# Last feed-forward stage: token scale moved into TensorE's turning, rounding constant taken off on ScalarE, normalisation on GpSimd

## The chip, the cores and the metric

One core of one Trainium2 chip. The metric is device time in microseconds of one execution of the whole program.

## The reference, cut to what matters

Eight layers (four attentions, four feed-forwards) work on `x` of 8 batches of 256 tokens of 256 values. The change is in the last layer, a feed-forward with quantised tokens, quantised weights and a depthwise convolution along the tokens:

```python
def act_quant(x):
    scale = 127.0 / jnp.clip(jnp.max(jnp.abs(x), axis=-1, keepdims=True), 1e-05)
    return jnp.clip(jnp.round(x * scale), -128, 127) / scale
...
h = bit_linear(x, w1)                                   # act_quant(x) @ weight_quant(w1).T
h = depthwise_conv1d(h.transpose(0, 2, 1), conv_w, conv_b)   # three taps along the tokens
h = h.transpose(0, 2, 1)
h = jax.nn.silu(h)
return bit_linear(h, w2)
...
x = x + _L3_ffn_ref(_layernorm(x, axis=-1), ...)
```

## The kernel before, in words

`build` runs the layers one after the other as stages; the last is `bit_ffn` (from line 2511). It works on one batch (256 tokens, two tiles of 128) at a time, in a pipeline of 12 steps. In step n, five batches are in work at once, each at another part of the layer:

- **batch n (new)**: VectorE normalises the two tiles (`norm`, line 2606, tile `xn`), takes the largest absolute value of each token (`token_scale`, line 2613, `amax`), makes of it the unit `qr` (line 2617) and its inverse `qs` (2619). ScalarE multiplies by `qs` and adds MAGIC = 1.5 x 2^23, which rounds to a whole number (`rounded`, 2714, `q1`).
- **batch n-1 (turn)**: VectorE takes MAGIC off and multiplies by `qr` (`unrounded`, 2627, `q2`, two instructions). TensorE turns the tokens (`turn_tokens`, 2808, `px`), ScalarE writes the high part (`high_part`, 2721, `xh`), VectorE the rest (`low_part`, 2632, `xl`).
- **batch n-2 (hid)**: for each of 8 groups f of 128 hidden channels TensorE multiplies (`hidden`, 2820, into one of three banks of `ph`), ScalarE applies the middle tap of the convolution (`middle_tap`, 2728), VectorE the first and the last (`first_tap` 2637, `last_tap` 2642, `y`). A bank is free again after its last tap. After f = 3 and f = 7 ScalarE applies the silu to half of the channels (`silu`, 2736, `sT`).
- **batch n-3 (end)**: for each of its two tiles TensorE turns the result (`turn_silu`, 2831, into the one buffer `pn`), VectorE finds the scale (`tile_scale`: 2651 `sax`, 2658 `sunit`, 2662 `sqs`), then `pn` is scaled and rounded to `s1`: tile 0 by ScalarE (`scaled`, 2743), tile 1 by VectorE (`scaled_late`, 2669, last in its step). GpSimd takes MAGIC off (`whole`, 2786 and 2790, `sq`). TensorE turns it back (`turn_back`, 2840, `pb`).
- **batch n-4 (last)**: ScalarE copies `pb` to `sqT` (`turned_back`, 2751), TensorE multiplies with the second weight (`product`, 2849, `po`), VectorE scales and adds it to `x` (`residual`, 2675). SyncE stores it.

Each engine runs its own list of a step in the order written out in its `step` function; nothing else orders the work, and every engine waits in order on semaphores. VectorE's list has 17 places: place 2f is the first tap of f, place 2f+1 its last tap, and the other operations are put at places:

```python
if turn and place < TB: unrounded(...)        # in front of the taps 0 and 1
if end and 3 <= place < 6: tile_scale(0)      # in front of the tap
if last and place in (6, 10): residual(...)
if new and place in (5, 6): norm(...)
if turn and place == 7: low_part(...)
if new and place in (9, 10, 12): token_scale(...)
```

ScalarE's and TensorE's lists go by f. TensorE, in front of `hidden(f)`: f = 2 `turn_silu` of tile 0; f = 3 `turn_tokens`, then `turn_back` of tile 1; f = 4 `product` of tile 0; f = 5 `product` of tile 1; f = 6 `turn_silu` of tile 1; `turn_back` of tile 0 at the end. ScalarE: f = 0 middle tap, `turned_back` of tile 0; f = 3 middle tap, `turned_back` of tile 1, `high_part`; f = 4 middle tap, `scaled`, `silu` of the first half; f = 7 middle tap, `rounded`, `silu` of the second half. Steps 0 to 3 and 8 to 11 are written out, 4 to 7 are a loop of two passes. Step 8 has no new batch, step 9 nothing to turn either, step 10 no hidden part, step 11 only the last part.

## Time and profile before

| | us |
|---|---|
| median of 3 runs | 1684.4 (1680.64 to 1686.13) |
| the profiled execution | 1677.31 |
| its span | 1675.4 |
| last feed-forward stage within the span | from 1529.7 to the end |
| VectorE busy in the span | 960.2 (57%) |
| TensorE, ScalarE, GpSimd busy | 1453.5, 648.3, 424.8 |
| granted TensorE clock, mean | 0.945 |

The span is the time from the first to the last instruction of the profiled execution. All times of the rows below are counted from its start. A timeline gives start, duration, engine, source line and tiles of each piece; a square bracket holds the idle time of the engine before it, and what ended it. The ends of matmuls are modelled, and a following matmul may start before them. VectorE's and ScalarE's instructions overlap by about 0.1 us too, so the distance of two starts is what one costs its engine.

### The profile page before, as it was taken

The page shows a single profiled execution, that of the slowest core. Times are in us where ns is not written, and L with a number is a line of the kernel's source. Part 1 is how long each engine was busy: PE and PEld are TensorE (multiplying, and loading weights), DVE is VectorE, ACT ScalarE, POOL GpSimd, SP SyncE. Part 2 cuts the span into 40 slices and gives each one's busy share as a digit, 9 for nine tenths or more (in the row PEclk, how much of TensorE's full clock was granted, in tenths as well). Part 3 has the DMA queues.
Part 4 walks back from the last instruction along what each step waited for, and adds up shares of the span by engine and source line. Part 5 has one row for each costly group of instructions (what it writes and reads, how often), then busy time and mean ns, then how long its engine had stood idle before and what let it go on. Part 6 is the DMA issues. An engine that isn't in the chain of part 4 may idle for free. (4 is left out here: it accounts for less than half of the span.)

```text
span 1675.4 us, 32751 instructions
## 1 busy us (share of the span) xinstructions
PE 1453.5 (87%) x11594; PEld 1275.4 (76%) x11594; DVE 960.2 (57%) x2376; ACT 648.3 (39%) x1422; POOL 424.8 (25%) x671
## 2 busy tenths in 40 slices
PE   4789998399986999999998789999999988885775
PEld 3456665389985788888887689999999986664664
DVE  4666763312213676666666565555555546776995
ACT  1233333022213444554544144444444422234773
POOL 2011101134304344344333011100000016650222
PEclk8899999599997999999999899999999999998897
...
DMA packets 97293, 139.82 MB, mean 83 GB/s; under 512 B 10080, under 2 KB 81248, under 8 KB 97056
## 3 DMA queue, kind: packets, MB, share of 16 engines
...
## 5 line engine op out<-in xcount | busy, mean ns | idle before, releaser
L1872 PE MATMUL f_ph<-f_xgT,f_w 128*128 128x128 f32 x2496 | 287.0, 276 | 2.8 <-ACT f_xgT L1906 2.3
L1872 PEld LDWEIGHTS f_ph<-f_xgT,f_w 128*128 128x128 f32 x2496 | 283.8, 193 | 3.4 <-issue 1.8
L1031 ACT ACTIVATE a_work<-a_ps,a_bias 128x128 f32<-128x128 f32 (+1 forms) x256 | 104.3, 420 | 172.2 <-issue 90.6
L1953 DVE TENSOR_TENSOR f_w_low<-f_w,f_w_high 128x2048 fp32r<-128x2048 f32 x39 | 89.4, 2293 | 99.8 <-ACT f_w_high L1912 99.8
L1231 POOL TENSOR_TENSOR a_work<-a_work,a_recip 128x256 f32<-128x256 f32 (+1 forms) x128 | 103.3, 829 | 146.9 <-DVE a_recip L1150 145.8
...
L574 DVE CUSTOM_DVE_ANT_0 a_shut_s<-a_ps,a_neg 128x256 f32<-128x256 f32 x256 | 93.1, 420 | 39.9 <-PE a_ps L253 39.3
L486 ACT ACTIVATE a_pT<-a_ps 128x1024 f32<-128x1024 f32 x64 | 65.6, 1025 | 119.4 <-PE a_ps L253 119.4
L1912 ACT ACTIVATE f_w_high<-f_w 128x2048 fp32r<-128x2048 f32 x39 | 74.5, 1910 | 85.4 <-DVE f_yg L1965 85.4
L1155 DVE TENSOR_TENSOR a_qk<-a_ps,a_qk 128x512 fp32r<-128x512 f32 x64 | 44.3, 692 | 96.8 <-ACT a_qk L1048 96.8
L1674 PEld LDWEIGHTS f_ph<-f_xgT,f_w 128*128 128x128 f32 x736 | 87.3, 195 | 6.5 <-DMA f_w<-in_f_w 4.0
L1674 PE MATMUL f_ph<-f_xgT,f_w 128*128 128x128 f32 x736 | 88.3, 279 | 3.6 <-DMA f_w<-in_f_w 2.7
L1883 PE MATMUL f_py<-f_w_high,f_h_high 128*128 128x256 f32 x312 | 91.4, 293 | 0.0
L1883 PE MATMUL f_py<-f_w_high,f_h_low 128*128 128x256 f32 x312 | 88.1, 282 | 0.0
L1958 DVE TENSOR_TENSOR f_h_low<-f_raw,f_h_high 128x512 fp32r<-128x512 f32 x78 | 56.9, 729 | 54.4 <-ACT f_h_high L1916 54.4
L1883 PE MATMUL f_py<-f_w_low,f_h_high 128*128 128x256 f32 x312 | 88.1, 282 | 0.0
L1916 ACT ACTIVATE f_h_high<-f_raw 128x512 fp32r<-128x512 f32 x78 | 49.2, 631 | 91.8 <-DVE f_raw L1973 91.8
L1684 PE MATMUL f_py<-f_w,f_hT 128*128 128x256 f32 x368 | 83.5, 380 | 0.0
L1755 DVE TENSOR_SCALAR f_hT<-f_ph,f_b 128x128 f32<-128x128 f32 x92 | 25.9, 344 | 87.8 <-PE f_ph L1674 87.8
L1684 PEld LDWEIGHTS f_py<-f_w,f_hT 128*128 128x128 f32 x368 | 68.1, 190 | 8.8 <-issue 0.2
L1716 ACT ACTIVATE f_hT<-f_ph,f_b 128x128 f32<-128x128 f32 x92 | 26.3, 368 | 121.5 <-PE f_ph L1674 121.5
L1132 DVE TENSOR_REDUCE a_top_s<-a_ps 128x2 f32<-128x256 f32 (+1 forms) x128 | 64.1, 542 | 2.6 <-PE a_ps L917 2.6
...
## 6 DMA issues: line engine op xcount, KB each, us to landing
...
```

Of the source, the lines that this page charges most:

```text
L486: act.activation(pT[:, u // 2 % 2, 2 * (u % 2):2 * (u % 2) + 2, :, :].rearrange("p j t n -> p j (t n)"), ps[:, ST:ST + 2, :], ACT.Exp, sca ...
L574: a = dve.tensor_tensor_reduce(out=shut_s[:, j, t, :], in0=ps[:, bank(m) + j, t * S:(t + 1) * S], in1=neg[:, m // U % 3, t, :], scale=1.0, ...
L1031: act.activation(prob[:, s, i, t * P:(P if t == 0 else TRI)], ps[:, SB + 2 * s + i, t * S:(t * S + P * (t + 1))], ACT.Exp, bias=bias[:, s, ...
L1132: dve.tensor_reduce(top_s[:, s, t, :], ps[:, SB + 2 * s:SB + 2 * s + 2, t * S:t * S + P * (t + 1)], AX.X, ALU.max).then_inc(max_done, 1)
L1231: pool.tensor_tensor(part, part, recip[:, s, t, :].unsqueeze(2).to_broadcast([P, 2, P * (t + 1)]), ALU.mult).then_inc(shares_done, 1)
L1674: mm = pe.matmul(ph[:, q, n, f * P:(f + 1) * P], w[:, s, k, (q * FQ + f) * P:(q * FQ + f + 1) * P], xgT[:, s, k, :], start=(k == 0), stop= ...
L1684: mm = pe.matmul(py[:, s, 0:D], hT[:, s, f, :], w2[:, s, f, :], start=(f == 0), stop=(f == FT - 1))
L1872: mm = pe.matmul(ph[:, q, n, f * P:(f + 1) * P], w[:, s, k, (q * FQ + f) * P:(q * FQ + f + 1) * P], xgT[:, s, k, :], start=(k == 0), stop= ...
L1883: mm = pe.matmul(py[:, s, 0:D], hT[a][:, s, f, :], w2_parts[b][:, s, f, :], start=(f == 0 and n == 0), stop=(f == FT - 1 and n == len(PASS ...
L1912: act.activation(w2_parts[0][:, s, :, :], w2[:, s, :, :], ACT.Copy).then_inc(w2_high, 1)
L1953: dve.tensor_tensor(w2_parts[1][:, s, :, :], w2[:, s, :, :], w2_parts[0][:, s, :, :], ALU.subtract).then_inc(w2_low, 1)
L1958: dve.tensor_tensor(hT[1][:, s, q * FQ:(q + 1) * FQ, :].rearrange("p f n -> p (f n)"), raw[:, q, :], hT[0][:, s, q * FQ:(q + 1) * FQ, :].r ...
```

## The change

GpSimd normalises the new tokens, as the first thing of its step, and leaves its loop: its 12 steps are written out. ScalarE takes MAGIC off right behind `rounded`, for both tiles in one instruction (`whole_tokens`); `q2` is then whole numbers. The unit `qr` is applied in the turning: GpSimd makes for each tile a 128x128 matrix with `qr` on its diagonal (`spread_scale`), and TensorE multiplies `q2` with it, where it had the identity. VectorE loses `norm` and `unrounded`; its other operations are put at other places. On TensorE, `product` of tile 0 goes from f = 4 to f = 3, ahead of `turn_tokens` and `turn_back`, and `product` of tile 1 from f = 5 to f = 6, behind `turn_silu` of tile 1. The diff, without the hunk that declares the tiles and semaphores:

```diff
@@ -2576,6 +2577,7 @@
         @block.vector
         def _(dve):
             dve.memset(magic[:, :], MAGIC).then_inc(magic_set, 1)
+            dve.memset(below[:, :], -MAGIC).then_inc(magic_set, 1)
             for i, part in enumerate((xh, xl)):
                 for end in (0, S + 1):
                     dve.tensor_scalar(part[:, :, :, end:end + 1],
@@ -2599,13 +2601,6 @@
             step(dve.tensor_scalar(total[:, :], diff[:, :], -0.5, 1.5, ALU.mult, ALU.add))
             step(dve.tensor_tensor(rstd[:, :], guess[:, :], total[:, :], ALU.mult))
 
-            def norm(pair, b, t):
-                row = pair * (2 * TB) + (b * TB + t)
-                if b >= 1:
-                    dve.wait_ge(q1_done, upto(pair, 2 * b - 1, 2))
-                dve.tensor_scalar(xn[:, t, :], x[:, row, :], mean[:, bass.ds(row, 1)], rstd[:, bass.ds(row, 1)],
-                                  ALU.subtract, ALU.mult).then_inc(xn_done, 1)
-
             def token_scale(pair, b, k):
 
                 if k == 0:
@@ -2614,18 +2609,12 @@
                 else:
                     dve.wait_ge(prep, upto(pair, 3 * b + k - 1, 3))
                 if k == 1:
+                    if b >= 1:
+                        dve.wait_ge(spread_done, upto(pair, 2 * b - 1, 2))
                     ins = dve.tensor_scalar(qr[:, :], amax[:, :], 1e-5, 1.0 / 127.0, ALU.max, ALU.mult)
                 if k == 2:
                     ins = dve.reciprocal(qs[:, :], qr[:, :])
                 ins.then_inc(prep, 1)
-
-            def unrounded(pair, b, t):
-
-                dve.wait_ge(q1_done, upto(pair, 2 * b + t, 2))
-                if b >= 1:
-                    dve.wait_ge(x_turned, upto(pair, b - 1))
-                dve.tensor_scalar(q2[:, t, :], q1[:, t, :], MAGIC, qr[:, t:t + 1], ALU.subtract, ALU.mult
-                                  ).then_inc(q2_done, 1)
 
             def low_part(pair, b):
                 dve.wait_ge(x_high, upto(pair, b))
@@ -2679,8 +2668,6 @@
 
                 new, turn, hid, end, last = (is_batch(n - i) for i in range(5))
                 for place in range(2 * FT + 1):
-                    if turn and place < TB:
-                        unrounded(pair, n - 1, place)
                     if end and 3 <= place < 6:
                         tile_scale(pair, n - 3, 0, place - 3)
                     if hid and place < 2 * FT:
@@ -2689,14 +2676,12 @@
                         tile_scale(pair, n - 3, 1, place - 12)
                     if end and place == 2 * FT:
                         scaled_late(pair, n - 3)
-                    if last and place in (6, 10):
-                        residual(pair, n - 4, (6, 10).index(place))
-                    if new and place in (5, 6):
-                        norm(pair, n, place - 5)
-                    if turn and place == 7:
+                    if last and place in (5, 11):
+                        residual(pair, n - 4, (5, 11).index(place))
+                    if turn and place == 6:
                         low_part(pair, n - 1)
-                    if new and place in (9, 10, 12):
-                        token_scale(pair, n, (9, 10, 12).index(place))
+                    if new and place in (7, 8, 10):
+                        token_scale(pair, n, (7, 8, 10).index(place))
 
             every_step(dve, step)
 
@@ -2704,15 +2689,21 @@
         def _(act):
             act.wait_ge(comb, 7)
             act.activation(root[:, :], vareps[:, :], ACT.Sqrt).then_inc(rooted, 1)
-            act.wait_ge(magic_set, 1)
+            act.wait_ge(magic_set, 2)
 
             def rounded(pair, b):
                 for t in range(TB):
                     act.wait_ge(prep, upto(pair, 3 * b + 2, 3))
                     if b >= 1:
-                        act.wait_ge(q2_done, upto(pair, 2 * b - 1, 2))
+                        act.wait_ge(q2_done, upto(pair, b - 1))
                     act.activation(q1[:, t, :], xn[:, t, :], ACT.Identity, bias=magic[:, 0:1], scale=qs[:, t:t + 1]
                                    ).then_inc(q1_done, 1)
+
+            def whole_tokens(pair, b):
+                act.wait_ge(q1_done, upto(pair, 2 * b + 1, 2))
+                if b >= 1:
+                    act.wait_ge(x_turned, upto(pair, b - 1))
+                act.activation(q2[:, :, :], q1[:, :, :], ACT.Identity, bias=below[:, 0:1]).then_inc(q2_done, 1)
 
             def high_part(pair, b):
                 act.wait_ge(x_turned, upto(pair, b))
@@ -2767,6 +2758,7 @@
                         silu(pair, n - 2, 0)
                     if new and f == 7:
                         rounded(pair, n)
+                        whole_tokens(pair, n)
                     if hid and f == 7:
                         silu(pair, n - 2, 1)
 
@@ -2775,7 +2767,25 @@
         @block.gpsimd
         def _(pool):
 
-            pool.wait_ge(magic_set, 1)
+            pool.wait_ge(magic_set, 2)
+
+            pool.wait_ge(comb, 12)
+
+            def norm(pair, b, t):
+                row = b * TB + t
+                if b >= 1:
+                    pool.wait_ge(q1_done, upto(pair, 2 * b - 1, 2))
+                pool.tensor_scalar(xn[:, t, :], x[:, row, :], mean[:, row:row + 1], rstd[:, row:row + 1],
+                                  ALU.subtract, ALU.mult).then_inc(xn_done, 1)
+
+            def spread_scale(pair, b):
+
+                pool.wait_ge(prep, upto(pair, 3 * b + 1, 3))
+                if b >= 1:
+                    pool.wait_ge(x_turned, upto(pair, b - 1))
+                for t in range(TB):
+                    pool.tensor_tensor(spread[:, t, :], ident[:, :], qr[:, t:t + 1].to_broadcast([P, P]), ALU.mult
+                                       ).then_inc(spread_done, 1)
 
             def whole(pair, b, t):
 
@@ -2791,21 +2801,30 @@
                                    ).then_inc(sq_done, 1)
 
             def step(pair, n):
-                for t in range(TB):
-                    if is_batch(n - 3):
-                        whole(pair, n - 3, t)
-
-            every_step(pool, step)
+                if is_batch(n):
+                    for t in range(TB):
+                        norm(pair, n, t)
+                if is_batch(n - 3):
+                    whole(pair, n - 3, 0)
+                if is_batch(n):
+                    spread_scale(pair, n)
+                if is_batch(n - 3):
+                    whole(pair, n - 3, 1)
+
+            for n in range(B + 4):
+                step(0, n)
 
         @block.tensor
         def _(pe):
             def turn_tokens(pair, b):
-                pe.wait_ge(q2_done, upto(pair, 2 * b + 1, 2))
+                pe.wait_ge(q2_done, upto(pair, b))
+                pe.wait_ge(spread_done, upto(pair, 2 * b + 1, 2))
                 if b >= 1:
                     pe.wait_ge(x_low, upto(pair, b - 1))
                 for k in range(DK):
                     for t in range(TB):
-                        mm = pe.transpose(px[:, k, t * P:(t + 1) * P], q2[:, t, k * P:(k + 1) * P], ident[:, :])
+                        mm = pe.matmul(px[:, k, t * P:(t + 1) * P], q2[:, t, k * P:(k + 1) * P], spread[:, t, :],
+                                       start=True, stop=True)
                 mm.then_inc(x_turned, 1)
 
             def hidden(pair, b, f):
@@ -2854,13 +2873,13 @@
                 for f in range(FT):
                     if end and f in (2, 6):
                         turn_silu(pair, n - 3, (2, 6).index(f))
-                    if last and f == 4:
+                    if last and f == 3:
                         product(pair, n - 4, 0)
                     if turn and f == 3:
                         turn_tokens(pair, n - 1)
                     if last and f == 3:
                         turn_back(pair, n - 4, 1)
-                    if last and f == 5:
+                    if last and f == 6:
                         product(pair, n - 4, 1)
                     if hid:
                         hidden(pair, n - 2, f)
```

## Rows read from the trace of the kernel before

**Rows 1.** Windows view, one stretch: us, busy time (instructions) of each engine, granted clock, DMA

```profile
1580.00:1590.00 10.00, 8.48 (x68) 7.57 (x68) 9.84 (x22) 7.71 (x12) 4.05 (x3) 0.92 0.00 0
```

**Rows 2.** Timeline of VectorE, steps 5 and 6: start us, duration us, engine, line, operation

```profile
1580.41 0.34 DVE L2627 TENSOR_SCALAR f_q<-f_q,f_qr 128x256 f32<-128x256 f32 x1
1580.88 0.48 DVE L2637 SCALAR_TENSOR_TENSOR f_y<-f_ph,t_cwu,f_y 128x256 f32<-128x256 f32 x1
1581.28 1.37 DVE L2627 TENSOR_SCALAR f_q<-f_q,f_qr 128x256 f32<-128x256 f32 x1
...
1595.15 0.34 DVE L2627 TENSOR_SCALAR f_q<-f_q,f_qr 128x256 f32<-128x256 f32 x1
...
1604.88 0.48 DVE L2637 SCALAR_TENSOR_TENSOR f_y<-f_ph,t_cwu,f_y 128x256 f32<-128x256 f32 x1 [0.29 <-ACT f_y L2728]
...
1610.27 0.34 DVE L2627 TENSOR_SCALAR f_q<-f_q,f_qr 128x256 f32<-128x256 f32 x1
```

**Rows 3.** Timeline of GpSimd, head of step 5

```profile
1580.57 1.93 POOL L2790 TENSOR_TENSOR f_sq<-f_s,f_magic 128x1024 bf16<-128x1024 f32 x1 [1.83 <-DVE f_s L2669]
```

**Rows 4.** Timeline of VectorE, the late scaling at the end of steps 7, 8 and 9

```profile
1623.82 1.27 DVE L2669 TENSOR_SCALAR f_s<-f_pn,f_sqs 128x1024 f32<-128x1024 f32 x1
...
1638.00 1.28 DVE L2669 TENSOR_SCALAR f_s<-f_pn,f_sqs 128x1024 f32<-128x1024 f32 x1
...
1652.14 1.28 DVE L2669 TENSOR_SCALAR f_s<-f_pn,f_sqs 128x1024 f32<-128x1024 f32 x1
```

**Rows 5.** Timeline of TensorE, steps 5 and 6

```profile
1582.70 0.66 PE L2808 MATMUL f_px<-ident,f_q 128*128 128x128 f32 x4
...
1583.62 0.49 PE L2820 MATMUL f_ph<-f_xh,t_w1q 128*128 128x258 f32 x2
...
1584.19 1.05 PE L2849 MATMUL f_po<-t_w2q,f_sqT 128*128 128x256 bf16 x8
1585.01 0.51 PE L2820 MATMUL f_ph<-f_xh,t_w1q 128*128 128x258 f32 x2
...
1588.55 1.04 PE L2831 MATMUL f_pn<-ident,f_sT 128*128 128x128 f32 x8
...
1599.16 0.49 PE L2820 MATMUL f_ph<-f_xh,t_w1q 128*128 128x258 f32 x2
```

**Rows 6.** Timeline of ScalarE, step 5

```profile
1580.30 0.55 ACT L2728 ACTIVATE f_y<-f_ph,t_fb,t_cwu 128x256 f32<-128x256 f32 x1
...
1585.75 0.60 ACT L2721 ACTIVATE f_xh<-f_px 128x512 fp32r<-128x512 f32 x1
...
1586.68 1.23 ACT L2743 ACTIVATE f_s<-f_pn,f_magic,f_sqs 128x1024 f32<-128x1024 f32 x1
```

**Rows 7.** Chain that ended last: start us, us on the chain, what

```profile
1560.10 0.59 DVE f_amax L2613
...
1587.75 0.60 DVE f_xl L2632
```

**Rows 8.** Timeline of an earlier stage (attention 1): a small VectorE operation beside GpSimd

```profile
705.77 1.61 POOL L1231 TENSOR_TENSOR a_work<-a_work,a_recip 128x256 f32<-128x256 f32 x2 [4.15 <-DVE a_recip L1150]
...
706.64 0.78 DVE L1135 TENSOR_SCALAR a_bias<-a_top_s 128x4 f32<-128x4 f32 x1
...
713.75 0.17 DVE L1135 TENSOR_SCALAR a_bias<-a_top_s 128x4 f32<-128x4 f32 x1
```

**Rows 9.** Timeline of VectorE, step 0 and the head of step 1

```profile
1532.96 0.73 DVE L2606 TENSOR_SCALAR f_xn<-x,f_mean,f_rstd 128x256 f32<-128x256 f32 x2
...
1535.55 0.85 DVE L2627 TENSOR_SCALAR f_q<-f_q,f_qr 128x256 f32<-128x256 f32 x2 [0.73 <-ACT f_q L2714]
```

**Rows 10.** Groups of GpSimd instructions by shape: count, busy us, mean ns, idle before

```profile
L1231 POOL TENSOR_TENSOR a_work<-a_work,a_recip 128x256 f32<-128x256 f32 x64 | 39.4, 616 | 146.9 <-DVE a_recip L1150 145.8
```

**Rows 11.** Timeline of the last step: ScalarE and TensorE

```profile
1666.19 1.02 ACT L2751 ACTIVATE f_sqT<-f_pb 128x1024 bf16<-128x1024 bf16 x1 [3.84 <-PE f_pb L2840]
...
1668.53 1.87 PE L2849 MATMUL f_po<-t_w2q,f_sqT 128*128 128x256 bf16 x8 [0.67 <-DVE x L2675]
```

7 lines of the change are left out of this document (4 added, 3 removed).

## The prediction

> **What bounds the kernel now.** I read the windows of the last stage first, because the change touches nothing else: in a stretch of 10 us VectorE is busy for 9.84, TensorE for 8.48, ScalarE for 7.71, GpSimd for 4.05 [rows 1]. So at first sight VectorE bounds the stage, and the change takes work from it. But a busy engine is a bound only if nothing else is nearly as late. So I looked next for steps that have less VectorE work. I count a step from the first `unrounded` of VectorE: step 5 takes 1595.15 - 1580.41 = 14.74 us, step 6 takes 15.12 [rows 2]. Where the new batch has run out, the late scalings lie 14.18 us apart (step 8, without `norm` and `token_scale`) and 14.14 (step 9, without `unrounded` and `low_part` as well) [rows 4]. Step 9 has some 4 us less for VectorE than step 5, and is 0.6 shorter. **So there is a second chain close behind VectorE.**
>
> Step 6 shows it. There the first tap of f = 5 waited 0.29 us for ScalarE [rows 2]. What ScalarE waits for is TensorE's `hidden(3)`: behind that come the middle tap of f = 3, `turned_back`, `high_part`, the middle tap of f = 4, `scaled`, `silu` and the middle tap of f = 5, all in ScalarE's order. `hidden(3)` started at 1599.16, 4.01 us after the start of the step [rows 2, 5]; the tap of f = 5 started at 1604.88, 5.72 later; from it to the end of the step VectorE takes 1610.27 - 1604.88 = 5.39 [rows 2]. So **the ring is: start of `hidden(3)` in the step + 5.72 + 5.39 = start + 11.11**. For step 6 that is 15.12. In step 5 `hidden(3)` started at 3.21 [rows 5], the ring gives 14.32, and VectorE's own work (14.74) ended last. The ring closes because TensorE's first turning in a step waits for the late scaling of the step before.
>
> **The change part by part.**
>
> *Off VectorE.* `unrounded`: the first takes 0.47 to the next start, but the tap behind it waits for the middle tap of f = 0, which ScalarE started only at 1580.30 and ended at 1580.85, just before the tap's 1580.88 [rows 2, 6]. Taking it away leaves that tap where it is. The second took 1.37 us, against 0.34, since GpSimd's `whole` ran from 1580.57 to 1582.50 [rows 2, 3]: some 1.3 us. The two `norm` start 0.37 apart (0.73 for two [rows 9]), so 0.7. In all 2.0 to 2.4 us a step, in a full step 12.3 to 12.7 us of VectorE's own work are left. Of this only 14.74 - 14.32 = 0.4 can be won before the ring binds. In steps 8 and 9 nothing is won: they are bound by it already.
>
> *TensorE's order.* `product` of tile 0 now stands ahead of `turn_tokens`, `turn_back` and `hidden(3)`. It costs 1585.01 - 1584.19 = 0.82 us [rows 5], before it lay behind `hidden(3)`, beside waits. Against this, `turn_tokens` started at 1582.70 [rows 5] only because of the blocked `unrounded`, and can now go 0.2 earlier. So `hidden(3)` starts at 3.21 + 0.82 - 0.2 = 3.84, and the ring becomes 3.84 + 11.11 = 14.95. `product` of tile 1 goes behind `turn_silu` of tile 1, ahead of `hidden(6)`. `turn_silu` waits for `scaled`. From the start of `hidden(3)` to the start of `high_part` are 1585.75 - 1583.62 = 2.13, from there to `scaled` 0.93, and `scaled` takes 1.23 [rows 5, 6]: with 0.07 to pass on 4.36. Then `turn_silu` (about 0.8 of its 1.04 before the next can start), `product` 0.82, `hidden(6)` and the middle tap (0.57 to the next start on TensorE, some 0.2 until its end, 0.55 on ScalarE [rows 5, 6]: 1.3), and from the first tap of f = 6 to the end 4.15 (the 5.39 less two taps and a residual at 0.4 each). Sum: 3.84 + 4.36 + 0.8 + 0.82 + 1.3 + 4.15 = 15.3 us.
>
> *The turning as a product.* Four matmuls of 128 columns instead of four turnings, `turn_tokens` 0.66 us now [rows 5]. No row has this pair of operands; the bounds are no more than now, and as much as doubled (+0.5 us on the ring). I take 0, because the transposes and plain products of float32 in this trace are alike in length.
>
> *ScalarE.* `whole_tokens`, one instruction of 512 columns: between the 0.60 of `high_part` [rows 6] and 0.85 (two `unrounded` on VectorE [rows 9]). In full steps it lies in ScalarE's wait ahead of the second `silu`, which the last tap of f = 7 ends: nothing. If that cover is gone, the middle tap of f = 0 is late by it.
>
> *GpSimd.* Two `norm`: between VectorE's 0.37 and 0.83 each (the 0.616 of rows 10, and a third more as an upper end). I take 0.55. Two `spread_scale` of 128 columns, at most the same 0.616 each [rows 10]. `whole` of the step before ends 2.1 us into the step [rows 3], both `norm` by 3.3, and VectorE wants them for `amax` after 6 us: covered. Being written out instead of looped costs nothing that a row shows, as GpSimd is 60% idle.
>
> *A new collision.* `token_scale` makes `qr` at place 8 (before: 10). In front of it, once `xh` is there, lie `low_part` 0.60, a tap 0.40, `amax` 0.59, a tap 0.40 [rows 2, 7]. So `qr` comes 0.60 + 0.03 + 1.99 = 2.6 us after the start of `high_part`. GpSimd's `whole` of tile 0 starts 0.93 + 1.23 + 0.07 = 2.2 after the same start, and lasts 1.9 [rows 3, 6]. **`qr` falls 0.4 us into it.** What that does is seen in the attention stage: a VectorE `tensor_scalar` of only four columns took 0.78 us, to the end of the GpSimd multiply that ran beside it, and 0.17 without one [rows 8]. `qr` has two columns, and no row has such a one beside GpSimd: the ends are 0 and the 1.5 us that remain of `whole`. I take 1.5, because rows 8 is nearest in kind. Then the step is: `hidden(3)` 3.84 + 2.13 + 2.23 + 1.93 = 10.1, and from the tap behind `qr` to the end 0.4 + 5.39: **15.9 us, 1.16 more than the 14.74 of now**.
>
> The Trainium skill bears on this point (SBUF — State Buffer, "Who interferes with whom", and VectorE: DVE Perf Modes, "Mode 2×_2P"): a `tensor_scalar` in SBUF whose outermost size is even takes the port pair that GpSimd needs too, and whichever starts first keeps it for its whole length. By this rule two columns are held up as four are, and the sum stays; without it the step would be 15.3.
>
> *Fill.* Step 0 is a bare chain: `norm` on GpSimd instead of VectorE 1.1 instead of 0.73, two hand-overs between engines 0.2 more, one more memset 0.06, `whole_tokens` behind both `rounded` instead of `unrounded` beside the second 0.35. In step 1 `whole_tokens` stands ahead of the first middle tap, some 0.5 more reach `hidden(3)`. Together +1.15. Step 3 has no `product`: 0.5 from VectorE, but the same collision, +0.4.
>
> *Drain.* Step 8 has no `qr`, but the order: +0.9. Step 9: +1.1. Step 10: `product` of tile 0 ahead of `turn_back`, whose result the rest waits for: +0.6. Step 11: `product` of tile 0 no longer waits behind `turn_back`, and that of tile 1 can start when `sqT` is ready, 1666.19 + 1.02 = 1667.21, instead of 1668.53 [rows 11]: -1.3.
>
> **Sum:** 1.15 + 0.4 + 4 x 1.16 + 0.9 + 1.1 + 0.6 - 1.3 = **+7.4 us**, 1677.3 to 1684.7 for the profiled execution. That execution was 7 us below the median of the runs shown, so against 1684.4 the forecast is 1691.8.
>
> **The rivals.** 0.3% (5 us) is about what a measurement of this kernel can tell from no change.
>
> 1. *`qr` passes freely* (two columns are not held up, or it comes before `whole`). The order of TensorE binds alone: 4 x (15.3 - 14.74) = 2.2 instead of 4.6, step 3 -0.3 instead of +0.4: +4.3, **1688.7**. For it: no row shows two columns blocked. Chance 0.27.
> 2. *The ring is looser, and a new order hides `product`.* Where TensorE reaches `turn_back` before `sq` of tile 1 is ready (2.1 us into the step), `product` fills a wait. The rate granted in rows 1 was 0.92, and a step whose head runs at the full one would give `hidden(3)` near 3.2 and the 0.4 us of gain: about 0 in all, **1684**. Chance 0.10.
> 3. *Faster: VectorE alone is the bound.* Then the 2.4 us come off five full steps, 12 us less the 1.2 of the fill: **1673.6**. For it: 9.84 of 10 us busy. Against it: steps 8 and 9. It decides if the first tap of f = 5 does not wait once VectorE is early. Chance 0.14.
> 4. *TensorE slow in every step as in step 6.* `hidden(3)` at 4.01 + 0.82, a step 16.9: **about 1697**. For it: TensorE idles longer in the new order. Chance 0.07.
>
> The forecast has 0.42. **Range** 1681 to 1698: it takes in cases 1, 2 and 4 and the bounds of `norm`, of the turning and of `qr`, and leaves out most of case 3. Faster by over 0.3%: 0.15 (case 3, and a little of 2). Within: 0.40 (most of 1 and 2, and the lower part of the forecast). Slower: 0.45.
>
> **What would show it.** Steps of 15.3 to 16 us between late scalings in steps 4 to 7; VectorE under 85% busy, waiting ahead of `low_part` for `xh`; `hidden(3)` at least 0.6 later in its step; `qr` with a duration over 1 us in steps 3 to 7 and its end at that of GpSimd's `whole`; `hidden(6)` behind `product`. Wrong if the steps fall under 14 us, if `qr` takes 0.16 everywhere, or if `low_part` starts without a wait.

## The result and the profile after

The changed kernel took 1699.66 us (median of 4 runs, 1697.4 to 1701.18) against 1682.52 for the kernel before (median of 4): the ratio is **1.0098, 95% interval 1.0074 to 1.0123**. The prediction was 1691.8, with a range up to 1698. So it is slower, as forecast, but by 17 us instead of 7, and the range was missed.

| | before | after |
|---|---|---|
| profiled execution, its span | 1677.31, 1675.4 | 1698.46, 1696.5 |
| start of the stage (first memset of VectorE) | 1529.74 | 1534.45 |
| stage, from there to the end of the span | 145.66 | 162.05 |
| VectorE, GpSimd, TensorE busy in the span | 960.2, 424.8, 1453.5 | 954.2, 449.2, 1464.5 |

The part of the program ahead of the stage is the same in both and varies by some us from run to run (in the profiled executions of all kernels here the stage starts between 1529.7 and 1538.7), so the *stage* is what is compared from here on: it grew by 16.4 us. Its steps are read from the late scalings, one per step. First the timeline of VectorE after, the late scalings of steps 3 to 7:

```profile
1573.31 1.27 DVE L2658 TENSOR_SCALAR f_s<-f_pn,f_sqs 128x1024 f32<-128x1024 f32 x1
1590.51 1.27 DVE L2658 TENSOR_SCALAR f_s<-f_pn,f_sqs 128x1024 f32<-128x1024 f32 x1
1607.40 1.28 DVE L2658 TENSOR_SCALAR f_s<-f_pn,f_sqs 128x1024 f32<-128x1024 f32 x1
1624.33 1.28 DVE L2658 TENSOR_SCALAR f_s<-f_pn,f_sqs 128x1024 f32<-128x1024 f32 x1
1641.33 1.27 DVE L2658 TENSOR_SCALAR f_s<-f_pn,f_sqs 128x1024 f32<-128x1024 f32 x1
```

Full steps take 16.9 to 17.2 us, where they took 14.74 to 15.11 [rows 2, 4]. Step 6 is the one in which the kernel before had its TensorE late, so I take it as the example. Some of its VectorE after, from the tap ahead of the wait for `xh` on:

```profile
1613.72 0.48 DVE L2626 SCALAR_TENSOR_TENSOR f_y<-f_ph,t_cwu,f_y 128x256 f32<-128x256 f32 x1
1615.11 0.69 DVE L2621 TENSOR_TENSOR f_xl<-f_px,f_xh 128x512 fp32r<-128x512 f32 x1 [0.92 <-ACT f_xh L2712]
...
1617.10 1.53 DVE L2614 TENSOR_SCALAR f_qr<-f_amax 128x2 f32<-128x2 f32 x1
...
1620.47 0.48 DVE L2664 SCALAR_TENSOR_TENSOR x<-f_po,f_sqr,x 128x256 f32 x1 [0.55 <-PE f_po L2868]
1621.44 0.48 DVE L2626 SCALAR_TENSOR_TENSOR f_y<-f_ph,t_cwu,f_y 128x256 f32<-128x256 f32 x1 [0.48 <-ACT f_y L2719]
```

VectorE is no longer the bound: it waits 0.92 us for `xh`, then 0.55 for `product`, then 0.48 for the middle tap of f = 6. `qr`, two columns, takes 1.53 us. GpSimd explains that length:

```profile
1616.71 1.89 POOL L2800 TENSOR_TENSOR f_sq<-f_s,f_magic 128x1024 bf16<-128x1024 f32 x1 [2.56 <-ACT f_s L2734]
```

It ends at 1618.60, and `qr` at 1618.63. But the wait that ends last is the one for the middle tap, and behind that stands TensorE, same step:

```profile
1612.35 0.49 PE L2839 MATMUL f_ph<-f_xh,t_w1q 128*128 128x258 f32 x2
...
1613.81 0.40 PE L2839 MATMUL f_ph<-f_xl,t_w1q 128*128 128x258 f32 x2
1616.68 1.94 PE L2850 MATMUL f_pn<-ident,f_sT 128*128 128x128 f32 x8 [2.47 <-ACT f_s L2734]
1618.41 1.90 PE L2868 MATMUL f_po<-t_w2q,f_sqT 128*128 128x256 bf16 x8
1619.98 0.58 PE L2839 MATMUL f_ph<-f_xh,t_w1q 128*128 128x258 f32 x2
```

With both products out of the way, TensorE has nothing between `hidden(5)` and `turn_silu` of tile 1, waits 2.47 us for `scaled`, and then `turn_silu` and `product` take 1.94 and 1.90 us, where rows of before show 1.04 and 1.05 for the same work [rows 5]. The windows view of just these stretches has the reason (length, busy time of each engine, granted clock, DMA):

```profile
1611.00:1614.20 3.20, 3.20 (x30) 2.87 (x28) 3.19 (x8) 1.09 (x2) 2.25 (x3) 1.00 0.00 0
1614.20:1616.60 2.40, 0.01 (x1) 0.00 (x0) 1.49 (x3) 2.40 (x5) 0.00 (x0) 1.00 0.00 0
1616.60:1620.00 3.40, 3.31 (x17) 2.83 (x17) 3.32 (x7) 1.44 (x3) 2.65 (x3) 0.52 0.00 0
1620.00:1621.70 1.70, 1.70 (x18) 1.52 (x16) 0.75 (x2) 0.86 (x2) 0.00 (x0) 0.95 0.00 0
```

TensorE worked without a break at the full 2.4 GHz until 1614.2, idled for 2.4 us, and the granted clock was 0.52, the lower level of 1.2 GHz, for the 3.4 us after. The Trainium skill (TensorE: Matmul & The Clock Gate, Part 1) describes a monitor that halves the array's clock when the engine has been idle; the rows agree in the two levels and in the fall after an idle stretch.

What else differs, by groups with shapes kept apart, after (count, busy us, mean ns, idle before):

```profile
L2778 POOL TENSOR_SCALAR f_xn<-x,f_mean,f_rstd 128x256 f32<-128x256 f32 x16 | 19.4, 1223 | 23.8 <-DVE f_rstd L2602 20.5 <-ACT f_q L2699 3.4
L2826 PE MATMUL f_px<-f_spread,f_q 128*128 128x128 f32 x64 | 10.2, 311 | 11.7 <-ACT f_q L2706 11.7
```

The `norm` takes 1.22 us on GpSimd, about three times VectorE's 0.37 [rows 9]. The turning by the diagonal is 64 matmul records where the turning with the identity had 32 for the same eight `turn_tokens`: two for each product.

**Where the 16.4 us are.** Predicted and measured, in differences from the kernel before, with three of the experiments below beside them (each step from late scaling to late scaling; the first line from the start of the stage):

| | predicted | after | before + order | after, order and `qr` as before | the same, turning, norm and `whole_tokens` undone too |
|---|---|---|---|---|---|
| fill to step 3 | +1.55 | +4.1 | +0.1 | +4.1 | +0.7 |
| steps 4 to 7 | +4.6 | +8.7 | +10.1 | +5.3 | +1.7 |
| step 8 | +0.9 | +3.2 | +2.3 | +1.0 | +0.4 |
| step 9 | +1.1 | -0.2 | +1.65 | -1.0 | -0.9 |
| step 10 | +0.6 | +1.85 | +3.25 | +0.6 | +0.6 |
| rest | -1.3 | -1.3 | -1.15 | +0.4 | -0.4 |
| stage | +7.5 | +16.4 | +16.3 | +10.4 | +2.0 |

### The profile page after: what moved, and what is told of

Same layout as the page of the kernel before. It is cut to its first block and busy times, and to the rows that moved or that the text cites. A ratio compares the mean times of both kernels' runs of the same rounds, so it can differ in the third digit from the quotient of the medians.

```text
span 1696.5 us, 32805 instructions
## 1 busy us (share of the span) xinstructions
PE 1464.5 (86%) x11626; PEld 1283.6 (76%) x11626; DVE 954.2 (56%) x2345; ACT 653.1 (38%) x1430; POOL 449.2 (26%) x703
```

## The experiments

Three accounts stood against each other. **The order:** it makes the second ring (through `turn_silu`, `product`, `hidden(6)`) the longest, as TensorE is at the lower clock after its wait. **The hold-up:** the late `qr` makes the step, as the prediction had it. **The small prices:** the turning, the `norm` and `whole_tokens`, put low or at nothing. "Stage" is that of each kernel's profiled execution; ratios are to the kernel before on the same chip. A stage is thus one execution per kernel, and how much it varies from one to the next wasn't measured. Where the intervals of two ratios overlap, a difference of their stages is one between two executions, to be explained by their rows, and isn't shown for the kernels' times.

Two distances explain most of what follows. In step 6 of the changed kernel the **head** (`turn_silu` of tile 0 and what stands up to `hidden(3)`) takes 3.75 us, and from `hidden(3)` to the end of the step it is 13.18. In the ring of the prediction the second distance was 11.11.

**1. The changed kernel, the product of tile 1 back ahead of `hidden(5)`.**

```diff
-                    if last and f == 6:
+                    if last and f == 5:
                         product(pair, n - 4, 1)
```

> The changed kernel with only the product of tile 1 back at f = 5, ahead of the turning of the silu of tile 1. Theory (TensorE's order binds: the product stands between the turning, which waits for ScalarE's scaling, and the hidden part f = 6, and both run at the low clock after a wait of 2.5 us): the wait at f = 6 gets shorter, hidden f = 6 follows the turning, full steps take 15.8 us instead of 16.9 to 17.2, all in all 5 to 8 us less than the changed kernel. Rival (the hold-up of qr by GpSimd binds): steps 4 to 7 stay within 0.3 us of 16.9, under 2 us less.

Measured: ratio 1.0097 [1.0079, 1.0115], stage 161.75, full steps 16.3, 16.7, 16.83, 16.96. Next to nothing, where my theory expected 5 to 8 us less. The rows show why, here step 6, which begins at 1604.97:

```profile
1609.83 0.49 PE L2839 MATMUL f_ph<-f_xh,t_w1q 128*128 128x258 f32 x2
```

```profile
1614.58 1.53 DVE L2614 TENSOR_SCALAR f_qr<-f_amax 128x2 f32<-128x2 f32 x1
...
1620.60 1.27 DVE L2658 TENSOR_SCALAR f_s<-f_pn,f_sqs 128x1024 f32<-128x1024 f32 x1
```

The wait ahead of `turn_silu` of tile 1 is 0.51 us now, it and the product of tile 1 run at the full clock (1.1 and 1.05 us), and VectorE does not wait once between `low_part` and the late scaling. So the second ring is gone, and the chain through the held-up `qr` sets the step. In the four full steps `hidden(3)` starts 4.33, 4.73, 4.86 and 5.0 us in, and each step is 11.97 longer than that, within 0.01. The prediction had 15.9 - 3.84 = 12.1 for this distance. What ate the gain is the head: `turn_silu` of tile 0 takes 1.94 and 1.97 us in steps 5 to 7, the lower clock again, where it took 1.07 and 1.09 in the changed kernel.

**2. The changed kernel, both products back** (also `f == 3` to `f == 4` for tile 0).

> The changed kernel with both products back at f = 4 and f = 5. Theory: hidden f = 3 starts 0.8 us earlier in its step, full steps take about 15.0 us (then bound by the hold-up of qr), about 10 us less than the changed kernel, so some 6 us more than the kernel before, most of it from the fill. Rival (hold-up of qr binds already): under 3 us less.

Measured: ratio 1.0072 [1.0046, 1.0097], stage 156.77, full steps 15.44, 16.24, 16.59, 16.85, and `qr` still 1.53 us in each of them. 5.3 us came back, half of what I expected. Again every step is `hidden(3)` (3.48, 4.27, 4.62 and 4.88 us in) plus 11.97: the hold-up is on the path, and the steps differ by their heads.

**3. The changed kernel, `token_scale` back at places 9, 10 and 12.**

```diff
-                    if new and place in (7, 8, 10):
-                        token_scale(pair, n, (7, 8, 10).index(place))
+                    if new and place in (9, 10, 12):
+                        token_scale(pair, n, (9, 10, 12).index(place))
```

> The changed kernel with token_scale back at places 9, 10 and 12, so that qr is made after GpSimd's whole of tile 0. Theory (TensorE's order binds, the hold-up lies beside it): qr takes 0.16 us again, steps stay at 16.7 to 17.2, under 2 us less. Rival (the hold-up is what lengthens the steps, as my prediction had it): full steps 15.3 to 15.8, 5 to 6 us less.

Measured: ratio 1.0132 [1.0107, 1.0158], stage 166.07; `qr` takes 0.16 us everywhere, and the full steps are 18.74, 18.07, 17.12, 17.06. **The hold-up is gone and nothing is gained.** Part of that is a price of the edit itself: `qs` comes later, and with it `rounded` and `whole_tokens`, so the second `silu` is late and `turn_silu` of tile 0 waits for it (0.25 to 0.81 us). `hidden(3)` starts 5.69, 6.49, 4.11 and 4.03 us into the full steps. But from there to the end of steps 4, 6 and 7 it is 13.05, 13.01 and 13.03, with `qr` at 0.16, against 12.9 to 13.2 in the changed kernel with `qr` at 1.53. The chain of TensorE lies beside the hold-up and is longer, so the hold-up falls as an account of the changed kernel.

Step 5 of this kernel shows what the clock alone is worth. There TensorE happened to stay at the full clock behind the same wait:

```profile
1603.20 1.09 PE L2850 MATMUL f_pn<-ident,f_sT 128*128 128x128 f32 x8 [2.64 <-ACT f_s L2734]
1604.13 1.04 PE L2868 MATMUL f_po<-t_w2q,f_sqT 128*128 128x256 bf16 x8
```

From `hidden(3)` to its end this step takes 11.58 us instead of 13.0, with the same order; the prediction had 11.4 for this distance.

**4. The changed kernel, `norm` on VectorE again (places 5 and 6).**

> The changed kernel with the normalisation back on VectorE at places 5 and 6. Theory: it matters in the fill only, where the two GpSimd instructions took 2.44 us and their start 0.8: the first largest value is found 2.6 us earlier, 2 to 3 us less in all, steps 4 to 7 within 0.3 us of 16.9. Rival (GpSimd's load of 9 us a step binds the steps too): more than 5 us less.

Measured: ratio 1.0113 [1.0096, 1.013], stage 164.24. The fill to step 3 is 37.83 instead of 38.86; steps 4 and 5 are 18.13 and 17.51 instead of 17.2 and 16.89, as `hidden(3)` starts 4.96 and 4.51 us in (4.28 and 3.8 in the changed kernel), behind a `turn_silu` of tile 0 of 1.97 and 1.77 us. Steps 6 and 7 are within 0.03 of the changed kernel. The 1.0 us of the fill is all that it gives, where I expected 2 to 3, and more is lost behind.

**5. The changed kernel with the tokens turned by transposes with the identity, as before.** The tokens' scale is left out of the result.

```diff
-                        mm = pe.matmul(px[:, k, t * P:(t + 1) * P], q2[:, t, k * P:(k + 1) * P], spread[:, t, :],
-                                       start=True, stop=True)
+                        mm = pe.transpose(px[:, k, t * P:(t + 1) * P], q2[:, t, k * P:(k + 1) * P], ident[:, :])
```

> The changed kernel with the tokens turned by transposes with the identity again, as before, so the scale of the tokens is left out of the result; everything else as in the change. Theory: the product of float32 with float32 is two instructions and costs 0.45 us more on TensorE than four transposes at the high clock, 0.9 at the low one. It lies on the path in the fill twice and ahead of hidden f = 3 in each step: 1 to 2 us less from the fill and 0.4 per step, 3 to 5 us less in all. Rival: TensorE waits for sq anyway, under 1.5 us.

Measured: ratio 1.0155 [1.013, 1.0179], stage 165.39. The turning itself is shorter and the kernel longer, where I expected it 3 to 5 us shorter. TensorE of this kernel in step 6, which begins at 1604.29: `turn_silu` of tile 0, `hidden(3)`, `turn_silu` of tile 1:

```profile
1604.43 1.97 PE L2849 MATMUL f_pn<-ident,f_sT 128*128 128x128 f32 x8 [0.41 <-DVE f_s L2658]
...
1608.88 0.48 PE L2838 MATMUL f_ph<-f_xh,t_w1q 128*128 128x258 f32 x2
...
1613.20 1.21 PE L2849 MATMUL f_pn<-ident,f_sT 128*128 128x128 f32 x8 [2.65 <-ACT f_s L2734]
```

The turning gives its 0.4 us back, but the head of steps 5 to 7 runs at the lower clock: the turning starts 3.61 to 3.97 us into the step, not 2.44 to 2.5, and `hidden(3)` 4.47 to 4.82, not 3.75 to 3.81. From there to the end it is 12.7 to 13.1 us, no more than in the changed kernel. The group of all `turn_silu` took 25.0 us in the stage instead of 23.5, and that of all products 24.0 instead of 22.0. So the shorter turning is paid for by more work at the lower clock. Why the clock is lower at the head here was not isolated.

**6. The kernel before with the order alone changed.**

```diff
-                    if last and f == 4:
+                    if last and f == 3:
                         product(pair, n - 4, 0)
                     if turn and f == 3:
                         turn_tokens(pair, n - 1)
...
-                    if last and f == 5:
+                    if last and f == 6:
                         product(pair, n - 4, 1)
```

> The kernel before with only the two products moved as the change moves them (tile 0 to f = 3, tile 1 to f = 6); nothing else of the change. Theory (the order is the main cost): steps 4 to 8 take 16.5 to 17.1 us instead of 14.2 to 15.1, the last step 1.3 less, in all +10 to +13 us against the kernel before, three quarters of the change's 17. Rival (the order costs only the 0.8 us of a product per step, and the rest comes from the hold-up, the normalisation and the turning): +2 to +5.

Measured: ratio **1.0132 [1.0113, 1.015]**, stage 161.97. Two moved lines, with nothing else of the change, cost as much as the whole of it, and more than the 10 to 13 us that I expected. Step 5 of this kernel on TensorE:

```profile
1599.14 1.71 PE L2831 MATMUL f_pn<-ident,f_sT 128*128 128x128 f32 x8 [2.30 <-ACT f_s L2743]
1600.63 1.92 PE L2849 MATMUL f_po<-t_w2q,f_sqT 128*128 128x256 bf16 x8
1602.20 0.78 PE L2820 MATMUL f_ph<-f_xh,t_w1q 128*128 128x258 f32 x2
```

and the stretch from 1599 on in the windows view:

```profile
1599.00:1602.20 3.20, 3.06 (x16) 2.58 (x17) 1.44 (x3) 1.48 (x3) 1.89 (x1) 0.57 0.00 0
```

The same picture. Here VectorE meets the late product as well, since `residual` of tile 1 is at place 10, not 11 as in the changed kernel:

```profile
1602.70 0.48 DVE L2675 SCALAR_TENSOR_TENSOR x<-f_po,f_sqr,x 128x256 f32 x1 [1.69 <-PE f_po L2849]
```

**7 and 8. The kernel before with one product moved: tile 0 to f = 3, or tile 1 to f = 6.**

> The kernel before with only the product of tile 0 moved from f = 4 to f = 3, ahead of the turnings and hidden f = 3. By the ring (start of hidden f = 3 in the step plus 11.1 us is the length of the step) hidden f = 3 moves back by the 0.8 us of a product: steps of 14.9 to 15.9 us, the last step 1.3 us less, +3 to +5 us in all. Rival (it fills a wait): within 1 us of the kernel before.

> The kernel before with only the product of tile 1 moved from f = 5 to f = 6, between the turning of the silu and hidden f = 6. Theory (the second ring: scaling, turning, product, hidden f = 6, tap f = 6, late scaling; and TensorE finds the low clock after the wait in front of the turning): steps of 16 to 16.9 us, +7 to +12 us. Rival (it costs its 0.8 us beside other work): +0 to +3.

Measured: tile 0 ratio 1.0039 [1.0015, 1.0062], stage 151.43 (+5.8); tile 1 ratio 1.0013 [0.9991, 1.0036], stage 148.53 (+2.9). Together they cost 16.3, and the two sum to 8.7: **7.6 us come only from the pair**. For tile 1 the expectation of 7 to 12 us missed and its rival (0 to 3) held; by the ratio its cost can't be told from none. With tile 0 moved, the first ring of the prediction can be read by itself: `hidden(3)` starts 4.36, 4.97, 3.98 and 4.92 us into the full steps, and these are 15.49, 16.08, 15.1 and 16.04 long, each 11.11 to 11.13 more. With tile 1 moved alone, `product` of tile 0 still stands behind `hidden(3)`, and the wait stays under 2 us. TensorE there:

```profile
1608.46 1.09 PE L2831 MATMUL f_pn<-ident,f_sT 128*128 128x128 f32 x8 [1.76 <-ACT f_s L2743]
1609.39 1.04 PE L2849 MATMUL f_po<-t_w2q,f_sqT 128*128 128x256 bf16 x8
```

After 1.76 us of waiting both are at full speed (granted clock 1.00 from 1608.4 to 1610.2).

**9. The order alone (as in 6), with 16 products whose result nobody reads, put into that wait.** They multiply the second weight with itself into the unused half of `po`.

```diff
+                    if end and hid and last and f == 6:
+                        pe.wait_ge(resid_done, upto(pair, TB * (n - 4), TB))
+                        for i in range(16):
+                            pe.matmul(po[:, D:2 * D], w2q[:, i % FT, 0:P], w2q[:, i % FT, :], start=True, stop=True)
                     if end and f in (2, 6):
                         turn_silu(pair, n - 3, (2, 6).index(f))
```

> The kernel before with both products moved (as in b_order), and 16 products without a use in the wait of TensorE ahead of the turning of the silu of tile 1 (in steps 4 to 9). They take about 1.7 us of a wait of 2.0 to 2.6. Theory (a part of the cost is the low clock after that wait): turning and product take 0.8 us each to the next start instead of 1.6, steps 1 to 1.6 us shorter than those of b_order, 5 to 8 us less than b_order. Rival (the order costs by its length alone): as b_order or longer.

Measured: 1693.95 us (6 runs), ratio **1.0045 [1.0018, 1.0072]** instead of 1.0132, stage 155.18 instead of 161.97. TensorE with the useless work:

```profile
1610.62 1.92 PE L2858 MATMUL f_po<-t_w2q 128*128 128x256 bf16 x16 [0.36 <-DVE x L2675]
1612.38 1.04 PE L2831 MATMUL f_pn<-ident,f_sT 128*128 128x128 f32 x8
1613.25 1.04 PE L2849 MATMUL f_po<-t_w2q,f_sqT 128*128 128x256 bf16 x8
1614.04 0.48 PE L2820 MATMUL f_ph<-f_xh,t_w1q 128*128 128x258 f32 x2
```

```profile
1612.40:1614.00 1.60, 1.60 (x17) 1.52 (x16) 1.37 (x3) 0.50 (x2) 1.07 (x1) 1.00 0.00 0
```

From the start of `turn_silu` to `hidden(6)` it is 1614.04 - 1612.38 = 1.66 us, against 1602.20 - 1599.14 = 3.06 in kernel 6. A kernel that got *more* work for TensorE became 6.8 us shorter in the stage. That settles the first account: a good part of what the wait costs is not the waiting but the clock behind it. From `hidden(3)` to the end of the step it is 11.57 to 11.59 us in steps 4, 5 and 7, against 13.10 to 13.25 in kernel 6. In step 6 it is 12.34, as the useless products themselves hold `turn_silu` up by 0.8 there. Some 9.5 us of the order's cost remain. In steps 4 to 7 `hidden(3)` starts 3.0 us later in all than before, which is `product` ahead of it and the head of the step, where `turn_silu` of tile 0 still ran at the lower clock in some steps of this kernel:

```profile
1619.78 1.94 PE L2831 MATMUL f_pn<-ident,f_sT 128*128 128x128 f32 x8
```

**10. The kernel before with `token_scale` at places 7, 8 and 10.**

> The kernel before with only token_scale moved from places 9, 10, 12 to 7, 8, 10. VectorE bounds its steps, so a hold-up of qr by GpSimd must show in full. If qr falls into GpSimd's whole of tile 0: its duration rises to between 0.5 and 1.9 us and each of steps 4 to 7 by the same, +2 to +7 in all. Rival (VectorE reaches it late enough, or two columns are not held up): qr 0.16 us, +0.

Measured: ratio 1.0031 [1.0013, 1.0049], stage 148.94 (+3.3). `qr` takes 0.6, 0.73, 1.52, 0.65 and 1.46 us in steps 3 to 7; steps 5 and 7 are 15.99 and 15.92 long, steps 4 and 6 15.19 and 15.1. So the hold-up is real, and where nothing longer lies beside it and it is met in full, a step pays about 1.2 us (15.99 and 15.92 against 14.75). That this is near the 1.16 of the prediction is chance, as that number had the later `hidden(3)` in it.

**11. The changed kernel with the order and `token_scale` as before.**

> The changed kernel with both products and token_scale back at their old places; normalisation on GpSimd, whole tokens on ScalarE and the turning with the scales stay. Theory: with the order undone, the hold-up of qr is what bounds, and taking it away too brings full steps to 14.1 to 14.4 us (the ring through ScalarE), 13 to 14 us less than the changed kernel, +2 to +4 against the kernel before, which is the fill. Rival (VectorE's relief counts): steps under 13.8 and faster than the kernel before.

Measured: 1689.83 us, ratio 1.0073 [1.0051, 1.0095], stage 156.04: both main suspects are gone, and 10.4 us are left, where 2 to 4 were expected. Full steps 16.73, 15.28, 15.99, 16.6. Step 6 on TensorE and ScalarE:

```profile
1603.46 1.71 PE L2850 MATMUL f_pn<-ident,f_sT 128*128 128x128 f32 x8 [0.81 <-ACT f_sT L2727]
...
1605.83 1.70 PE L2826 MATMUL f_px<-f_spread,f_q 128*128 128x128 f32 x8
1607.37 0.61 PE L2859 MATMUL f_pb<-identb,f_sq 128*128 128x128 bf16 x8
1607.79 0.49 PE L2839 MATMUL f_ph<-f_xh,t_w1q 128*128 128x258 f32 x2
```

```profile
1617.65 0.72 ACT L2706 ACTIVATE f_q<-f_q,f_below 128x512 f32<-128x512 f32 x1
1618.28 1.04 ACT L2727 ACTIVATE f_sT<-f_y 128x1024 f32<-128x1024 f32 x1
```

The turning takes 1.70 us at the lower clock; from its start to `hidden(3)` it is 1607.79 - 1605.83 = 1.96, where it was 1583.62 - 1582.70 = 0.92 before [rows 5]. `hidden(3)` starts 1607.79 - 1602.97 = 4.82 into the step, and the ring of the prediction (+ 11.11) gives 15.93 for the measured 15.99. And `whole_tokens` stands ahead of the second `silu` when the last tap has ended (1617.36 + 0.48 = 1617.84): the cover that the prediction gave it is gone. It is gone because `token_scale` went back: `rounded` waits for `qs`, which comes later; in the changed kernel and in kernel 2 the second `silu` still waits for the last tap. So against kernel 2 this one gains 0.8 us a step behind `hidden(3)` (11.17 instead of 11.97) and loses 0.7 ahead of it, in the mean of the full steps. This left the small prices open, in three parts.

**12 to 15. Kernel 11 with one more part undone each, and with all three.** 12: turning by transposes (diff of 5; the tokens' scale is left out). 13: `whole_tokens` in the next step. 14: `norm` on VectorE. 15: all three (the tokens' scale is left out). What is left of the change then is that ScalarE's `whole_tokens` does the work of VectorE's `unrounded`; besides, GpSimd still makes the diagonals, and `residual` and `low_part` keep their new places on VectorE.

```diff
                     if hid:
                         middle_tap(pair, n - 2, f)
+                    if turn and f == 1:
+                        whole_tokens(pair, n - 1)
...
                     if new and f == 7:
                         rounded(pair, n)
-                        whole_tokens(pair, n)
```

> The changed kernel with the order of TensorE and token_scale as before, and besides the turning of the tokens by transposes with the identity (this leaves the tokens' scale out of the result). Without the last edit the stage took 156.04 us, and the turning 1.70 us in a step whose head ran at the lower clock. Theory (the rest is a sum: turning, whole_tokens, fill): the turning takes 0.66 to 0.9 us, hidden(3) starts that much earlier, and seven steps in which the ring binds gain 0.5 to 0.9 each: stage 150 to 152.5 us. Rival (the head of a step at the lower clock costs what the turning happens to stand in, and would be paid anyway): under 2 us, stage over 154.

> The changed kernel with the order of TensorE and token_scale as before, and besides whole_tokens out of ScalarE's place ahead of the second silu, into the next step behind the middle tap of f = 1. Stage so far 156.04 us. Theory: the second silu started 1618.28 there, 0.44 us behind the last tap it needs, since whole_tokens (0.72) stood in front; now it starts at once, turn_silu(0) starts 0.4 earlier, and on four or five full steps that is 1.6 to 2.5 us; the fill gives 0 to 0.4: stage 153.5 to 154.5. Rival: the middle tap of f = 2 is late by the 0.72 in its place and the gain is given back: 156 or more.

> The changed kernel with the order of TensorE and token_scale as before, and besides the norm back on VectorE. Stage so far 156.04 us. Theory: the fill gains the 1.0 us that it gained when the same was undone alone, and a full step, bound by TensorE, neither gains nor loses (VectorE has waits ahead of low_part): stage 154.5 to 155.5. Rival (VectorE is the bound again once the order is as before): each full step 0.7 longer, stage 157 to 158.

> All three at once: the order of TensorE and token_scale as before, turning by transposes (the tokens' scale is left out of the result), whole_tokens in the next step behind the middle tap of f = 1, norm on VectorE. What is left of the change is that VectorE no longer makes unrounded. Theory (sum of parts): 156.04 less 4.5 for the turning, 2 for whole_tokens, 1 for the norm: stage 148 to 149, at most 3 over the 145.7 of before, and the time within 0.3% of before. Rival (something else of the change costs, such as the unrolled order on GpSimd or the two spread_scale): stage over 151.

| kernel | ratio, 95% interval | stage | fill to step 3 | steps 4 to 7 |
|---|---|---|---|---|
| 11 | 1.0073 [1.0051, 1.0095] | 156.04 | 38.8 | 16.73, 15.28, 15.99, 16.6 |
| 12, turning | 1.0031 [1.0012, 1.005] | 150.98 | 37.82 | 14.98, 15.93, 14.89, 15.89 |
| 13, `whole_tokens` | 1.006 [1.0031, 1.0088] | 154.25 | 40.53 | 15.52, 15.2, 15.51, 15.21 |
| 14, `norm` | 1.0055 [1.0026, 1.0083] | 156.74 | 37.17 | 15.89, 16.41, 16.76, 16.87 |
| 15, all | 1.0025 [1.0003, 1.0047] | 147.7 | 35.43 | 14.84, 15.54, 14.85, 15.78 |

Undoing the turning is worth 5.1 us here, `whole_tokens` 1.8 (3.2 in the four full steps, less 1.7 that the fill was longer), the `norm` -0.7 alone (the fill gained 1.6, full steps lost 1.3, step 10 1.25), and all three 8.3. Only for the turning and for all three do the ratios bear it out; those of kernels 13 and 14 can't be told from kernel 11, and 14 has the lower ratio with the longer stage. Full steps of all five are the start of `hidden(3)` plus 11.16 to 11.33 us: the first ring. In kernel 12 the turning's groups are

```profile
L2826 PE MATMUL f_px<-ident,f_q 128*128 128x128 f32 x32 | 6.7, 350 | 11.7 <-ACT f_q L2706 11.7
```

against, in kernel 11,

```profile
L2826 PE MATMUL f_px<-f_spread,f_q 128*128 128x128 f32 x64 | 12.8, 367 | 11.7 <-ACT f_q L2706 11.7
```

6.1 us less in eight turnings, 5.1 of them in the stage: nearly the whole of it was on the path. Kernel 15 is within 2.0 us of the stage before, so nothing large is left unexplained. **But with `unrounded` off VectorE and nearly all else undone, it is not faster than before either**: steps of 14.84 to 15.78. The relief of VectorE, which is what the change was for, brought nothing in any kernel tried here; one in which VectorE loses `norm` and `unrounded` and no other engine gets work ahead of `hidden(3)` was not among them.

**16. The kernel before, rearranged to keep `unrounded` from GpSimd's `whole`:** `unrounded` at places 3 and 4, `turn_tokens` ahead of the product of tile 1 at f = 5, `high_part` at f = 5, `low_part` at place 12.

```diff
-                    if turn and place < TB:
-                        unrounded(pair, n - 1, place)
+                    if turn and place in (3, 4):
+                        unrounded(pair, n - 1, place - 3)
...
-                    if turn and place == 7:
+                    if turn and place == 12:
                         low_part(pair, n - 1)
...
-                    if turn and f == 3:
+                    if turn and f == 5:
                         high_part(pair, n - 1)
...
-                    if turn and f == 3:
-                        turn_tokens(pair, n - 1)
...
+                    if turn and f == 5:
+                        turn_tokens(pair, n - 1)
                     if last and f == 5:
                         product(pair, n - 4, 1)
```

> The kernel before with work taken out of the ring and away from GpSimd's whole: unrounded at VectorE's places 3 and 4 (after whole of tile 1 has ended), turning of the tokens at f = 5 on TensorE, high part at f = 5 on ScalarE, low part at place 12. Theory: unrounded takes 0.34 us every time (0.95 less a step on VectorE), the ring loses 1 us of turning and high part; steps 4 to 7 take 14.0 to 14.3 us instead of 14.7 to 15.1, 2 to 4 us less than the kernel before in all. Rival (another chain as close behind): steps as before, within 1 us.

Measured: 1681.28 us (12 runs) against 1684.19 (31 runs), ratio 0.9983 [0.9965, 1.0002]: no difference that can be told. Both `unrounded` take 0.34 us, GpSimd never holds VectorE up, and the steps are still 14.84 to 15.32. At the head of each step VectorE now waits for the middle taps of f = 0 and f = 1, a time that the two `unrounded` had filled; behind them the profile shows no wait in steps 4, 6 and 7, and in step 5 one for ScalarE. First that one, then the head of step 6:

```profile
1591.09 0.48 DVE L2637 SCALAR_TENSOR_TENSOR f_y<-f_ph,t_cwu,f_y 128x256 f32<-128x256 f32 x1 [0.66 <-ACT f_y L2728]
...
1597.55 0.48 DVE L2637 SCALAR_TENSOR_TENSOR f_y<-f_ph,t_cwu,f_y 128x256 f32<-128x256 f32 x1 [0.39 <-ACT f_y L2728]
...
1598.91 0.48 DVE L2637 SCALAR_TENSOR_TENSOR f_y<-f_ph,t_cwu,f_y 128x256 f32<-128x256 f32 x1 [0.36 <-ACT f_y L2728]
```

So of the 0.95 us that the edit was to take off VectorE, 0.75 come back as waiting.

## Why the prediction was right and wrong

**What held.** VectorE is not the only bound: it waits in three places after, and the 12 us of the third rival did not come (nor in kernels 15 and 16). `hidden(3)` starts 1612.35 - 1608.60 = 3.75 us into step 6 (the step begins 1.20 after the start of the late scaling at 1607.40); predicted 3.84. That is partly luck: the turning took 0.4 us more than predicted, and the head ran at the full clock (`turn_silu` of tile 0 1.09 us, 1.55 in step 5 before), which gave as much back. `xh` follows 2.13 later, as before; `turn_silu` of tile 1 starts at 8.08, predicted 3.84 + 4.36 = 8.20. `low_part` waits for `xh`, and VectorE is busy for 14.16 of the 16.9 us of step 6. `qr` is held up in every full step until GpSimd's `whole` ends, to 10.03 us into step 6, predicted 10.1. So the rule of the Trainium skill (SBUF — State Buffer, "Who interferes with whom"; VectorE: DVE Perf Modes, "Mode 2×_2P") holds for two columns as well: 1.53 us beside `whole`, 0.16 without. `whole_tokens` at 0.72 lay between its bounds. The rest behind step 10 gained 1.28 us, predicted 1.3: `product` of tile 1 now starts right after `sqT`.

**The step that failed: the second ring.** The prediction had "`turn_silu` (about 0.8 of its 1.04 before the next can start), `product` 0.82", and from there 1.3 + 4.15 to the end. The last part measured 5.55 (from 1619.98 to the end of the step at 1625.53), predicted 5.45. The first two measured 1618.41 - 1616.68 = 1.73 and 1619.98 - 1618.41 = 1.57. Put in, 3.75 + 4.33 + 1.73 + 1.57 + 5.55 = 16.93, the step's measured length. **The ring was right in its members and wrong in one rate: both durations were taken from rows at the full clock, though the same edit that put them in a row also emptied the wait ahead of them.** That makes the second ring (16.9) longer than the chain through `qr` (3.75 + 11.97 = 15.7 with the distance of kernels 1 and 2), which is why the hold-up costs nothing in the changed kernel. Once the order is undone (kernels 1 and 2) it binds. Step 5 of kernel 3 and kernel 9 show the clock as the cause: with it at the full level the distance behind `hidden(3)` is 11.6 us, with it at the lower one 13.0 to 13.2. Over steps 4 to 7 the difference is 8.7 - 4.6 = 4.1 us, in step 8, which has no `qr` but the same order, 2.3, in step 10 1.25.

The prediction weighed a slow TensorE in its rival 4 and came to 1697 with a chance of 0.07. It had the slow TensorE at the head of the step ("TensorE idles longer in the new order") and not at its middle. Its step of 16.9 is the measured length by chance: it was `hidden(3)` at 4.83 and the chain through `qr`, which is what kernels 1 and 2 turned out to be (4.86 and 16.83 in step 6 of kernel 1), not the changed kernel. The clock should have been asked of every wait that the new order opens.

**The fill** (+4.1, predicted +1.15, and +0.4 for step 3). To the first `amax` it is 1541.04 - 1534.45 = 6.59 us, where the same distance before was 1533.73 - 1529.74 = 3.99: +2.6. GpSimd after:

```profile
1538.49 2.44 POOL L2778 TENSOR_SCALAR f_xn<-x,f_mean,f_rstd 128x256 f32<-128x256 f32 x2 [20.48 <-DVE f_rstd L2602]
```

Two `norm` take 2.44 us where I took 1.1, above even my upper bound of 0.83 each. That bound came from a multiply of two tensors of the same size, and the operation with two per-token scalars takes twice as long as that. The first starts 0.83 after VectorE's `rstd` (1537.49 + 0.17) ends. Then the turning at the lower clock:

```profile
1544.12 2.07 PE L2826 MATMUL f_px<-f_spread,f_q 128*128 128x128 f32 x8 [11.72 <-ACT f_q L2706]
```

2.07 us against 1.12 before: +0.95. `whole_tokens` gave +0.37 (predicted 0.35). Together 3.9, all of it before the first `hidden`; the rest of steps 0 to 3 added 0.2, predicted 0.9. The sum of the fill was also added up wrongly: its terms (0.37, 0.2, 0.06, 0.35 and 0.5) make 1.48, not 1.15, and the terms of the whole as written make 7.5, not 7.4. Put right, the forecast would have been 1692.2.

**The turning** was taken at 0 "because the transposes and plain products of float32 in this trace are alike in length". Each one is; but a plain product of full float32 is *two* of them. The upper bound (doubled, +0.5) was right at the full clock (1.06 us, [rows 5] 0.66) and is +1.0 at the lower one. It stands ahead of `hidden(3)`, and so in both rings: in full steps of the changed kernel it costs 0.4 us, hidden by the head at the full clock as said above, and with order and `token_scale` undone 5.1 us in all.

**Sum.** The 8.9 us that the forecast of the stage missed are 4.1 in steps 4 to 7, 2.3 and 1.25 in steps 8 and 10, 2.6 in the fill, less 1.3 in step 9, which I had put at +1.1 without a working and which became 0.2 shorter. There the head ran at the full clock, 1.07 us for `turn_silu` of tile 0 against 1.72 before, and `turn_silu` of tile 1 started 6.76 us into the step instead of 7.50, which paid for the product behind it. What the parts cost does not add: the order alone +16.3, all the rest without order and early `qr` +10.4, all together +16.4, as each step takes the longest of several chains that lie within 1 to 2 us of each other.

**What stays open.** Full steps of kernels 12 and 15 alternate between 14.9 and 15.9 us. In kernel 12 the head of both runs at the lower clock, but in the longer one (step 7) already `hidden(0)` does, 0.80 us for its first pair against 0.51, and it lasts until `turn_back`:

```profile
1619.61 0.80 PE L2838 MATMUL f_ph<-f_xh,t_w1q 128*128 128x258 f32 x2 [2.21 <-DVE f_y L2631]
...
1625.54 1.00 PE L2858 MATMUL f_pb<-identb,f_sq 128*128 128x128 bf16 x8
```

What sets it earlier in one step than in the next wasn't tried. And of the 9.5 us of the order that stay with the useless products in place, how much is the head of the step and how much `product` ahead of `hidden(3)` wasn't separated. More widely, the head of the step runs at the lower clock in some steps of nearly every kernel here and moves a step by up to 1 us; what decides it is open, and it makes any price of 1 to 2 us that is read from a single execution uncertain.
